# A post-norm decoder layer on one core: scores as 64-row by 32-column tiles of bfloat16 parts, one shared pool of seven PSUM banks

## The chip, the core and the metric

The kernel runs on one NeuronCore of a Trainium2 chip. TensorE multiplies, VectorE (DVE) and ScalarE (ACT) empty PSUM and do the element-wise work, GpSimd (POOL) does masks and small pieces, SyncE (SP) issues DMAs. The metric is device time in microseconds (us) of one execution.

## What is computed

Four sequences of 256 tokens with 128 channels go through self-attention, cross-attention and a small MLP, each followed by a residual add and a layer norm. Both attentions have 16 heads of 8 channels. Cut to what matters:

```python
# 1: latent self-attention, causal over 256 keys
k_eff, v_eff = (W_dq.T @ W_uq.T @ W_uk), (W_uv.T @ W_o.T)      # folded weights
c_kv = x @ W_dkv.T; q = x @ W_dq.T @ W_uq.T
attn = softmax(causal(q_heads @ k_eff @ c_kv.T / sqrt(8)))
x = layernorm(x + heads(attn @ c_kv @ v_eff))
# 2: cross-attention, keys = 512 of memory (ctx) + 256 of x, causal over the 256
q = x @ Wq; k, v = split(concat(mem, x) @ Wkv)
x = layernorm(x + heads(softmax(mask(q @ k.T / sqrt(8))) @ v) @ Wout + bout)
# 3: per-feature MLP: 64 features, 16 inner units each
s = x @ Win + bin_                      # 64 features
h = relu(s[..., None] * W1 + b1)        # 64 x 16
x = layernorm(x + (einsum('btmh,mh->btm', h, W2) + b2) @ Wout + bout)
```

## The kernel before, in words

The work is 8 units: units 0 to 3 are the self-attention of sequences 0 to 3 ("kind 1"), units 4 to 7 their cross-attention ("kind 2"). Each unit has 4 steps, and a step t is one unit and one group of four heads, so there are 32 steps: 16 of kind 1 with 256 keys, 16 of kind 2 with 768 keys.

A step computes its scores twice. First with queries on the partitions ("max", lines 1043 to 1078), so that DVE can take each query's maximum over the keys (lines 866 and 869). The maxima are transposed on TensorE ("shift", line 1084), copied out by ACT (line 744), and sent by two small DMAs (line 600) into two extra rows of the query operand `qm`. Then the scores are computed again with keys on the partitions ("exp", lines 1086 to 1108), where the two extra rows subtract the maximum inside the product, and ACT takes the exponential of each 512-wide bank into `probs` (line 735). Values times weights ("pv", line 1122) are float32 products whose stationary operand is 128 rows by 9 columns (8 channels and a column of ones for the sum); four heads go side by side into the four 32-column strips of the array. ACT copies the result out (`headsT`, line 750, the "drain", one per step), TensorE transposes it by a product ("norm", line 1130), and DVE divides by the sum (lines 888 and 892).

Operand layout of the scores: a head has 8 channels. For accuracy each query and key is split into a high and a low float32r part, and three products of parts are stacked as 3 x 8 rows. Four heads of a group are stacked, which gives 96 rows; `qm` holds for each head a copy with zeros in the rows of the other heads. So a product uses 96 or 98 rows and 128 columns of the array for one head (or, in "exp", streams two heads of queries one after the other). The spreading of the parts over the rows goes through DRAM scratch (`scr_q1`, `scr_k1`, `scr_m`, `scr_q2`, `scr_k2`: written by `put`, lines 530 to 534, read by `take_keys` and `take_queries`, lines 536 to 546).

PSUM has 8 banks: three for "max", two for "exp", one for the heads, two for everything else. The causal masks are bfloat16 products that add a large negative number (lines 1077 and 1108), except in kind 2 of "exp", where GpSimd zeroes the weights (line 669).

The order on all engines comes from a planner, `schedule()` (lines 128 to 354): it simulates the engines with costs per stage and writes one list of stages that every engine walks in order. Ahead of that list stands a prologue written by hand (lines 576 to 595, 715 to 717, 813 to 825, 1015 to 1031): weight folds, the q, k and v products of self-attention, the first memory keys, and memsets of `qm` and `ks` on GpSimd; line 821 prepares an MLP operand on DVE. A step can start once its queries and keys have come back from DRAM. The remaining products of memory are "late" jobs in the list.

The MLP of a sequence: `s` (line 1172) is split into high and low (lines 932 to 936), a selection product copies each feature to its 16 inner units (line 1180), ACT (line 779) or DVE (lines 946 and 951) applies W1, b1 and relu, and lines 1189 and 1197 go back to 128 channels.

## Time and profile before

| | |
|---|---|
| median of 3 runs | 309.77 us (309.51 to 310.59) |
| span of the profiled execution | 309.5 us |
| TensorE (PE) busy | 277.4 us, 90% of the span |
| DVE busy | 234.5 us, 76% |
| ACT busy | 174.3 us, 56% |
| GpSimd busy | 72.6 us, 23% |

In rows of the profile, PE is a matmul and PEld the load of its stationary operand; busy time of a group is the union of its instructions, "mean ns" the length of one including its way through the array, so overlapping instructions make the sum of means larger than the busy time. What stands behind "idle before" is the time the engine waited just before such instructions, and what released it.

### The profile page before, as it was taken

Reading aid. Unit: us, or ns where it says so; the run is one execution under the profiler, and the core shown is the slowest. Engines: PE = TensorE matmul, PEld = TensorE weight load, DVE = VectorE, ACT = ScalarE, POOL = GpSimd, SP = SyncE. Lnnn points to the kernel's source line nnn. Section 1 sums busy time; section 2 is a strip of 40 time slices with the busy share of each in tenths; the row PEclk is TensorE's granted clock in tenths of the full one; section 3 lists DMA queues with packets and bytes.
Section 4 is the critical chain, followed back from the end, with each engine's and each line's share of the span. In section 5 each row is a group of like instructions: output and inputs, shape, how many; then the busy total and the mean of one; then the engine's idle time right before and its main releaser. Section 6 shows DMA issues by size and latency. Waiting matters only on the chain.

```text
span 309.5 us, 6148 instructions
## 1 busy us (share of the span) xinstructions
PE 277.4 (90%) x2240; PEld 181.3 (59%) x2240; DVE 234.5 (76%) x540; ACT 174.3 (56%) x365; POOL 72.6 (23%) x108
## 2 busy tenths in 40 slices
PE   4918678899999999999999999999999999999762
PEld 3706566576776657665656565665665666554431
DVE  2797716587775998888889878799778799777463
ACT  1520235456556567756667566776676658667430
POOL 8996601001202020301111211013101112112211
PEclk9985969999999999999999999999999999999795
DMA  6669999302034512120006200033000000000001
GB/s 188 243 190 303 258 300 229 137 3 55 4 124 85 175 35 102 54 103 3 1 2 162 48 1 2 1 86 71 2 3 2 2 2 1 3 2 17 2 18 34
DMA packets 16109, 23.64 MB, mean 76 GB/s; under 512 B 1648, under 2 KB 11824, under 8 KB 15952
## 3 DMA queue, kind: packets, MB, share of 16 engines
q1 hardware_dynamic: 13632, 14.19, 16.4%
q0 software_dynamic: 2160, 7.47, 8.0%
q10 hardware_dynamic: 288, 1.59, 1.4%
q8 instruction: 18, 0.29, 0.4%
q14 instruction: 11, 0.09, 0.1%
HBM read 13.02 MB, written 9.96 MB: 74 GB/s over the span
## 4 chain that ended last, share of the span: by engine, by line
PE 72%; DVE 17%; DMA 3%; issue 3%; SPq 1%; ACT 1%; POOL 0%; POOLq 0%; ACTq 0%; DVEq 0%
PE psum L1122 15%; PE psum L1104 13%; PE psum L1067 9%; PE psum L1075 7%; DVE pmax L869 5%; PE psum L1077 4%; PE psum L1130 4%; PE psum L1106 4%; DVE w2x L821 3%; DMA qm<-shift_rows 3%; PE psum L1084 3%; PE psum L1108 2%; DVE nmax_s L880 2%; DVE nmax_s L881 2%; PE psum L1159 1%
## 5 line engine op out<-in xcount | busy, mean ns | idle before, releaser
L735 ACT ACTIVATE probs<-psum 128x512 f32<-128x512 f32 x224 | 127.1, 594 | 61.0 <-PE psum L1104 36.1
L869 DVE TENSOR_REDUCE pmax<-psum 128x1 f32<-128x512 f32 (+2 forms) x176 | 111.9, 682 | 19.6 <-PE psum L1067 10.4
L1104 PE MATMUL psum<-qm,ks 98*128 98x512 f32 x176 | 79.9, 463 | 0.0
L1122 PE MATMUL psum<-probs,v 128*9 128x256 f32 (+1 forms) x1024 | 60.6, 354 | 0.0
L1075 PE MATMUL psum<-ks,qm 96*128 96x128 f32 (+1 forms) x256 | 51.0, 309 | 8.2 <-DVE probs L810 8.2
L1067 PE MATMUL psum<-ks,qm 96*128 96x512 f32 x128 | 52.6, 424 | 0.0
L1075 PEld LDWEIGHTS psum<-ks,qm 96*128 96x128 f32 x256 | 43.1, 202 | 13.1 <-issue 9.6
L866 DVE TENSOR_REDUCE nmax<-psum 128x2 f32<-128x512 f32 (+1 forms) x48 | 31.8, 687 | 18.4 <-PE psum L1077 18.3
L1104 PEld LDWEIGHTS psum<-qm,ks 98*128 98x128 f32 x176 | 33.1, 191 | 17.5 <-ACT probs L735 13.3
L669 POOL TENSOR_SCALAR_AFFINE_SELECT probs<-probs 128x512 f32<-128x512 f32 x32 | 19.7, 634 | 96.5 <-ACT probs L735 96.5
L1122 PEld LDWEIGHTS psum<-probs,v 128*9 128x9 f32 x1024 | 21.7, 90 | 31.2 <-issue 9.4
L1077 PE MATMUL psum<-neg,ident_b 128*128 128x256 bf16 (+1 forms) x96 | 31.9, 332 | 0.0
L1106 PE MATMUL psum<-qm,ks 98*128 98x512 f32 x48 | 23.8, 514 | 6.1 <-issue 4.5
L1067 PEld LDWEIGHTS psum<-ks,qm 96*128 96x128 f32 x128 | 24.1, 190 | 4.9 <-DVE pmax L869 1.7
L674 POOL TENSOR_SCALAR vpe<-moments 128x2 f32<-128x2 f32 x12 | 2.6, 218 | 103.5 <-DVE moments L840 103.5
L744 ACT ACTIVATE shift_rows<-psum 8x256 fp32r<-8x256 f32 x32 | 11.8, 368 | 18.2 <-PE psum L1084 14.0
L1130 PEld LDWEIGHTS psum<-wa_sb,headsT 128*128 128x128 f32 x128 | 18.0, 191 | 2.0 <-issue 0.3
L1130 PE MATMUL psum<-wa_sb,headsT 128*128 128x36 f32 x128 | 17.5, 261 | 0.1
L750 ACT ACTIVATE headsT<-psum 128x256 f32<-128x256 f32 x32 | 12.3, 383 | 8.3 <-PE psum L1122 8.1
L1108 PE MATMUL psum<-negT,ident_b 128*128 128x256 bf16 (+1 forms) x48 | 15.9, 332 | 0.0
L1084 PE MATMUL psum<-wa_sb,nmax_s 128*8 128x128 f32 x64 | 12.2, 272 | 2.7 <-DVE nmax_s L881 2.7
L1106 PEld LDWEIGHTS psum<-qm,ks 98*128 98x128 f32 x48 | 9.8, 204 | 8.0 <-issue 5.3
(133 smaller groups left out, 291.4 us busy)
## 6 DMA issues: line engine op xcount, KB each, us to landing
qm<-scr_q SPq DMA_DIRECT2D x28, 96.0 KB
ks<-scr_k SPq DMA_DIRECT2D x6, 384.0 KB, 4.4
ks<-scr_m POOLq DMA_DIRECT2D x2, 768.0 KB, 7.6
ks<-scr_m SPq DMA_DIRECT2D x2, 768.0 KB, 6.4
ctxT_sb<-ctxT ACTq DMA_DIRECT2D x1, 1024.0 KB, 8.2
scr_m<-probs POOLq DMA_DIRECT2D x2, 512.0 KB, 7.1
qm<-shift_rows SPq DMA_DIRECT2D x64, 4.0 KB
scr_k<-split_k SPq DMA_DIRECT2D x4, 256.0 KB, 2.0
```

Of the source, the lines that this page charges most:

```text
L735: nc.scalar.activation(probs[:, ring % PRING, h:h + nh, q0:T], src, ACT.Exp, scale=SCALE).then_inc(exp_done, 1)
L866: nc.vector.tensor_reduce(nmax[:, t % 2, col:col + nh], tile, axis=AX.X, op=ALU.max, negate=True).then_inc(max_done, 1)
L869: nc.vector.tensor_reduce(pmax[:, t % 2, col:col + nh, part], tile, axis=AX.X, op=ALU.max).then_inc(max_done, 1)
L1067: last = nc.tensor.matmul(sk, lhs(j), ks2[0:STACK, b % 2, g, 0:MEM], start=True, stop=True)
L1075: nc.tensor.matmul(o, lhs(j + k), keys, start=(k == 0), stop=False)
L1077: last = nc.tensor.matmul(tile, ident_b[:, :], neg[:, 0:nh, :], start=False, stop=True)
L1084: last = nc.tensor.transpose(m[0:2 * HG, qt * P:(qt + 1) * P], nmax_s[:, t % 2, qt, :], ident)
L1104: nc.tensor.matmul(tbank[n % TBANKS], keys, queries, start=True, stop=True).then_inc(scoresT_ready, 1)
L1106: nc.tensor.matmul(tbank[n % TBANKS], keys, queries, start=True, stop=False)
L1108: nc.tensor.matmul(tile, ident_b[:, :], negT[:, 0:nh, :], start=False, stop=True).then_inc(scoresT_ready, 1)
L1122: last = nc.tensor.matmul(obank[t % OBANKS][32 * j:32 * j + HS + 1, q0:T], v, probs[:, pv_no[s] % PRING, j, q0:T], start=(kt == 0), stop=( ...
L1130: last = nc.tensor.matmul(m[:, qt * HG * (HS + 1):(qt + 1) * HG * (HS + 1)], headsT[:, t % 2, qt * P:(qt + 1) * P], used_rows, start=True, ...
```

## The change

The program is rewritten around the scores:

- Scores. The float32r parts (high, low) become three bfloat16 parts (high, middle, low), and six products of parts are stacked as 6 x 8 = 48 rows, plus three rows for the maximum (in three bfloat16 parts, under ones), so a head takes 51 of 64 rows. Even heads lie on partitions 0 to 63, odd heads on 64 to 127. A score product is issued as four matmuls, each 32 stationary columns wide, into the four column strips of the array (`in_tiles`). No copies padded with zeros are kept.
- "max" becomes "S": a memory unit is one head, 128 queries by 512 keys (4 matmuls); an own unit is one head, both query tiles, 128 + 256 key columns and a 256-column mask (12 matmuls). "exp" becomes "T": one key tile and two heads of the same half, 512 or 256 columns, 8 matmuls, and 4 more for the mask in kind 1.
- "pv" keeps its form: 128 rows, 9 columns, float32.
- PSUM: one bank for the heads, and seven shared by all other stages; the planner assigns the bank and the stage that must be emptied before.
- The splitting of maxima moves from DVE to GpSimd (four small operations a step). "norm" is done once a unit (8 products of 36 columns) instead of once a step. The third part of queries and keys is made on GpSimd. In kind 1 the two row DMAs are issued by ACT, not SP.
- Prologue: most of it is moved into the planned list; only the weight folds stay ahead. The memsets of `qm` and `ks` and the DVE preparation on line 821 are gone. Small filler products ("warm") are added at the start and in planned gaps of TensorE.
- MLP: W1 and b1 become the stationary operand of a float32 product over one 32-row strip (17 rows used), so relu is the only thing left for ACT or DVE, on 512 columns at once.
- A new planner with new costs.

The diff, cut to its core:

```diff
+PARTS = 3
+SLOTS = 6
+STRIP = 32
+HALF = P // 2
+DATA = SLOTS * HS
+ROWS = DATA + PARTS
+FREE_BANKS = 7
+HEADS_BANK = 7
+PRING = 8
+ROWBUFS = 4
...
+LATE = [(("qk", 0), 0), (("qk", 1), 0), (("v1", 0), 0), (("qk", 2), 0), (("v1", 1), 0),
+         (("m", 0), 2), (("vm", 0), 4), (("qk", 3), 6), (("m", 1), 8), (("vm", 1), 10), (("m", 2), 16), (("vm", 2), 17),
+         (("m", 3), 20), (("vm", 3), 21)]
...
+def s_units(t):
+    own = [("own", j, 0) for j in range(HG)]
+    return own if kind(t) == 1 else [("mem", 2 * a + r, qt) for a in range(2) for qt in range(QT) for r in range(2)] + own
...
+                    if what == "qk":
+                        scr = scr_qk[n]
+                        sp.dma_start(scr[:, 0:3, :, :], parts).then_inc(put_done[i], 16)
+                        sp.dma_start(scr[:, 3:5, 0, :], parts[:, 0:4:2, :]).then_inc(put_done[i], 16)
+                        sp.dma_start(scr[:, 3:5, 1, :], parts[:, 3:6:2, :]).then_inc(put_done[i], 16)
+                        sp.dma_start(scr[:, 5, :, :], parts[:, 0::5, :]).then_inc(put_done[i], 16)
...
+                    if i == 0:
+                        sp.dma_start(ctxT_sb[:, :], ctxT).then_inc(ctxT_in, 16)
+                        sp.dma_start(x_sb[:, :, :], x_rows.rearrange("(n p) c -> p n c", p=P)).then_inc(x_in, 16)
...
+                    nc.gpsimd.tensor_copy(high, full).then_inc(max_step, 1)
+                    nc.gpsimd.tensor_sub(rest, full, high).then_inc(max_step, 1)
+                    nc.gpsimd.tensor_copy(mid, rest).then_inc(max_step, 1)
+                    nc.gpsimd.tensor_sub(low, rest, mid).then_inc(max_split, 1)
...
+                    nc.scalar.activation(probs[:, ring % PRING, r, 0:cols], bank_of(s)[:, 0:cols], ACT.Exp,
+                                         scale=SCALE).then_inc(exp_done, 1)
...
+                elif what == "rows" and rows_on_act(s[1]):
+                    send_rows(act, s[1])
...
+                    if src == "mem":
+                        nc.vector.tensor_reduce(pm[:, place, 1 + 4 * qt:2 + 4 * qt], m, axis=AX.X, op=ALU.max).then_inc(reduced, 1)
+                    else:
+                        nc.vector.tensor_reduce(pm[:, place, 2:5], own_blocks(m), axis=AX.X, op=ALU.max).then_inc(reduced, 1)
...
+            def in_tiles(o, lhs, rhs, start, stop):
+                for c in range(HG):
+                    last = nc.tensor.matmul(o[STRIP * c:STRIP * (c + 1)], lhs[:, STRIP * c:STRIP * (c + 1)], rhs, start=start,
+                                            stop=stop, skip_group_check=True)
+                return last
+            def mask(o, r, rows):
+                for c in range(HG):
+                    last = nc.tensor.matmul(o[STRIP * c:STRIP * (c + 1)], half(unit_b, r, HALF), half(rows, r, HALF)[:, c, :, :],
+                                            start=False, stop=True, skip_group_check=True)
+                return last
+            def score(s):
+                queries, keys = (half(qk[:, u % B, p, a, :], r, DATA) for a in range(2))
+                m = bank_of(s)
+                if src == "mem":
+                    return in_tiles(m, queries[:, qt * P:(qt + 1) * P], half(km[:, u % B, p, :], r, DATA), True, True)
+                in_tiles(m[:, 0:P], queries[:, 0:P], keys[:, 0:P], True, False)
+                in_tiles(m[:, P:P + T], queries[:, P:T], keys, False, False)
+                return mask(own_blocks(m)[:, 0:3:2, :], r, neg)
+            def score_pair(s):
+                for a in range(2):
+                    last = in_tiles(m[:, a * (T - q0):(a + 1) * (T - q0)], keys, half(qk[:, u % B, p, 0, q0:], r, ROWS),
+                                    a == 0 or not masked, not masked)
...
+                    elif what == "hid":
+                        for k in range(2):
+                            inner = strip(wb_sb, j, FS + 1)[:, WB["w1"] + k * P:WB["w1"] + (k + 1) * P]
+                            last = nc.tensor.matmul(m[:, k * T:(k + 1) * T], inner, strip(s_sb, j, FS + 1), start=True, stop=True)
-                        last = nc.tensor.matmul(m[:, k * T:(k + 1) * T], sel_r[:, f * P:(f + 1) * P], feat_s[b], start=True, stop=True)
...
-            for s in pro:
-                if s in split_jobs:
-                    low_half(s, bank(pro_bank[s]))
...
-                    for f in range(FG):
-                        last = nc.vector.tensor_scalar(w2x[:, f, :], wb_sb[:, WB["place"] + 32 * f:WB["place"] + 32 * f + 32],
-                                                       wb_sb[:, WB["w2"] + f:WB["w2"] + f + 1], None, ALU.mult)
```

## Rows read from the trace of the kernel before

**Rows 1.** The page: engines over the span, and the chain by engine.

```profile
PE 277.4 (90%) x2240; PEld 181.3 (59%) x2240; DVE 234.5 (76%) x540; ACT 174.3 (56%) x365; POOL 72.6 (23%) x108
PE 72%; DVE 17%; DMA 3%; issue 3%; SPq 1%; ACT 1%; POOL 0%; POOLq 0%; ACTq 0%; DVEq 0%
```

**Rows 2.** Drains (ACT, timeline): start, length; of steps 0, 15 and 31.

```profile
54.79 0.38 ACT L750 ACTIVATE headsT<-psum 128x256 f32<-128x256 f32 x1 [0.20 <-PE psum L1122]
...
121.47 0.38 ACT L750 ACTIVATE headsT<-psum 128x256 f32<-128x256 f32 x1 [0.20 <-PE psum L1122]
...
285.47 0.39 ACT L750 ACTIVATE headsT<-psum 128x256 f32<-128x256 f32 x1
```

**Rows 3.** Windows between those drains: engines busy (instructions), clock, DMA share, GB/s.

```profile
24.00:55.00 31.00, 25.14 (x147) 18.91 (x147) 17.70 (x37) 10.49 (x29) 11.55 (x19) 0.77 0.97 275
55.00:121.50 66.50, 65.31 (x582) 44.95 (x581) 50.84 (x135) 39.27 (x87) 6.41 (x13) 1.00 0.26 79
121.50:285.50 164.00, 161.46 (x1378) 100.61 (x1378) 138.93 (x307) 110.34 (x217) 27.62 (x50) 1.00 0.10 27
285.50:309.50 24.00, 13.30 (x88) 7.93 (x88) 11.42 (x40) 7.24 (x16) 4.57 (x10) 0.75 0.06 17
```

**Rows 4.** TensorE timeline within a kind 2 step: start, length, instructions merged.

```profile
203.47 0.40 PE L1104 MATMUL psum<-qm,ks 98*128 98x512 f32 x1
203.71 0.40 PE L1067 MATMUL psum<-ks,qm 96*128 96x512 f32 x1
204.04 0.84 PE L1122 MATMUL psum<-probs,v 128*9 128x256 f32 x16
204.81 0.50 PE L1104 MATMUL psum<-qm,ks 98*128 98x512 f32 x1
205.14 0.40 PE L1067 MATMUL psum<-ks,qm 96*128 96x512 f32 x1
```

**Rows 5.** Those pv instructions (line 1122), window 203 to 205: min/median/max ns.

```profile
L1122 PE MATMUL psum<-probs,v x16: 272/326/385, 204.0 to 204.6; 128*9 128x256 f32 x8, 128*9 128x128 f32 x8
```

**Rows 6.** Groups by shape: busy us, mean ns of one, idle before.

```profile
L735 ACT ACTIVATE probs<-psum 128x512 f32<-128x512 f32 x224 | 127.1, 594 | 61.0 <-PE psum L1104 36.1 <-PE psum L1108 23.1
L869 DVE TENSOR_REDUCE pmax<-psum 128x1 f32<-128x512 f32 x128 | 81.8, 682 | 10.8 <-PE psum L1067 10.4
L1077 PE MATMUL psum<-neg,ident_b 128*128 128x256 bf16 x64 | 18.8, 294 | 0.0
L1130 PE MATMUL psum<-wa_sb,headsT 128*128 128x36 f32 x128 | 17.5, 261 | 0.1
L1077 PE MATMUL psum<-neg,ident_b 128*128 128x512 bf16 x32 | 13.1, 408 | 0.0
L880 DVE CAST nmax_s<-nmax 128x8 fp32r<-128x8 f32 x32 | 9.5, 297 | 1.1
```

**Rows 7.** The two waits of TensorE's sequencer ahead of that pv pair (line 1116), window 203.2 to 203.5.

```profile
L1116 PEldq EVENT_SEMAPHORE  x2: 51/51/51, 203.3 to 203.4; - x2
```

**Rows 8.** A 256-column float32 product in the chain: start, share of the chain in us.

```profile
83.45 0.43 PE psum L1159 x2
```

**Rows 9.** The prologue and the first exponential (timeline): start, length.

```profile
4.08 0.38 ACTq L699 DMA_DIRECT2D wb_sb<-wb  x1
8.81 0.38 ACT L713 ACTIVATE probs<-psum 128x256 fp32r<-128x256 f32 x1 [2.56 <-PE psum L1004]
12.01 11.51 DVE L821 TENSOR_SCALAR w2x<-wb_sb 128x32 f32<-128x32 f32 x8
26.16 0.69 DVE L866 TENSOR_REDUCE nmax<-psum 128x4 f32<-128x512 f32 x1 [0.59 <-PE psum L1077]
41.57 1.26 ACT L735 ACTIVATE probs<-psum 128x512 f32<-128x512 f32 x2 [5.84 <-PE psum L1108]
```

**Rows 10.** DMA issues on the page: count, KB each, us from issue to landing.

```profile
ks<-scr_k SPq DMA_DIRECT2D x6, 384.0 KB, 4.4
ctxT_sb<-ctxT ACTq DMA_DIRECT2D x1, 1024.0 KB, 8.2
```

1766 lines of the change are left out of this document (844 added, 922 removed).

## Prediction, written before the changed kernel was run

> **What bounds the kernel now.** I read the page first. TensorE is busy 90% of the span and carries 72% of the chain that ended last, DVE 17% [rows 1]. That busy time includes the way through the array, so it must be checked stage by stage. The drains mark the stages: the first ends a start-up of 54.8 us, the sixteenth comes at 121.5, the thirty-second at 285.5, and 24.0 us follow [rows 2]. Between them the windows show the load [rows 3]:
>
> - start-up, up to 54.8 us: nobody is full but the DMA engines, 0.97 of their time at 275 GB/s from 24 to 55 us, at a TensorE clock of 0.77 granted;
> - kind 1, 15 steps in 66.7 us, 4.45 us each: TensorE 65.3 of 66.5 us, DVE 50.8, ACT 39.3;
> - kind 2, 16 steps in 164.0 us, 10.25 us each: TensorE 161.5, DVE 138.9, ACT 110.3;
> - tail, 24.0 us, a chain of small stages.
>
> So per step of kind 2 TensorE needs 10.1 us, DVE 8.7, ACT 6.9 (the row divided by 16). TensorE is the bound, but DVE stands only 15% below: removing TensorE work can bring a step down to DVE's 8.7 and no further. The sum is made against the profiled span of 309.5 us; the median of the runs is 309.8, so I add 0.3.
>
> **What a score costs on TensorE.** 512 columns of float32r follow each other at 0.24 us (203.47 to 203.71) [rows 4]. The bfloat16 masks cost 294 ns for 256 columns and 408 for 512 [rows 6]; the difference, 0.114 us per 256 columns, is the same rate. So going to bfloat16 gains nothing per column: all gain must come from two heads at once, one in each half of the rows. Columns in a kind 2 step: before, 8 x 512 (memory), 2560 (own, with masks) and 11 x 512 (exp) = 12288. After: S 8 x 512 + 4 x 640, T 10 x 512 + 2 x 256 = 12288 again. At 0.114 us per 256 that is 5.5 us if the halves take turns, 2.75 us if they always overlap.
>
> Do they overlap? For column strips rows show it: the 16 pv instructions take 272 to 385 ns each, 326 in the median [rows 5], 5.2 us one after another, and all lie within 0.84 us [rows 4]. Row halves are not used before, so their overlap is bounded from both sides, 0 and 100%. I take 85%: it is the same kind of tile as the strips, S and T units alternate between halves in the planned order and each has a bank of its own; and the overlap regulates itself, because when TensorE is late more banks are empty and more pairs can go together. The other 15% is for units that wait for a bank or have a stage of another form between them. Score time after: 5.5 x (1 - 0.85/2) = 3.2 us. Before: 19 x 0.24 + 2560 columns (1.1) = 5.7 us. Saved: 2.5 us a step.
>
 Taking 0.2 us for each (they share the way with pv when adjacent), +0.5 us; bounds 0 and 0.75 for as many, 2.5 us for eight more.
>
> **pv** is unchanged. **norm**: the same 128 instructions, 17.5 us [rows 6], in eight lumps instead of 32; nothing. **Shift**: at most as long as before; nothing.
>
> **MLP on TensorE.** 16 selections of 2 x 256 columns in float32r (0.23 us) become float32 products; one of 256 columns takes 0.43 us [rows 8], so a pair 0.86, or 0.43 if K of 17 rows makes it cheaper; +0.2 to +0.63 us for each of four a unit. Taken +0.4 us a step.
>
> Kind 2 on TensorE: 10.1 - 2.5 + 0.5 + 0.4 = 8.5 us, bounds 8.0 (full overlap, no more switches) and 11.5 (no overlap, 2.3 us: 10.8; and the larger switch and MLP values).
>
> **DVE.** Reduced columns are the same: 128 memory units as before, 81.8 us for 128 [rows 6], 0.64 each; own units are 128 x 384 instead of 96 x 512, equal columns, 32 instructions more, each of which adds the fixed part of one (0.64 minus 512 columns; taking a quarter, 0.11 us), 3.5 us in all. The split of the maxima leaves DVE: 9.5 us on line 880 [rows 6] and as many instructions on line 881; each norm saves little. Relu is one instruction of 512 columns (before, four of 256 on DVE) and can go to ACT. Net -1 us a step in kind 2 before balancing, but DVE also waits less in start-up and can run ahead of T in kind 1. Per step: 7.7 to 8.7 us. The split on GpSimd lengthens the way from the last maximum to the rows by about 1 us; GpSimd is busy 27.6 of 164 us [rows 3], and T lags S by several steps' worth of banks, so it is hidden; if that cover is gone it costs 1 us a step in kind 1 only.
>
> **ACT.** Exponentials: 224 of 512, 127.1 us [rows 6], 0.567 each; after, 192 of 512 (108.9) and 64 of 256. The latter cost 0.567 minus half its columns, 0.30: 19.2. Sum 128.1, +1.0 us. Kind 1 adds two DMA issues a step at 0.38 [rows 9], 0.8 us, to ACT's 39.3/15 = 2.6: 3.4, still below 4.2. In kind 2 ACT takes most copies of the MLP: 6.9 + 1 = 7.9 us.
>
> So in kind 2 all three stand between 7.7 and 8.7 us. Three engines that near to each other do not reach 100% of the largest; before, with one clear bound, the step was 10.25 against 10.1. I take **9.1 us a step**, 16 x 9.1 = 146 us (bounds 8.5 and 9.9).
>
> **Kind 1.** Before, the scores of a step are 2560 + 2048 columns (with masks), 2.05 us, and some 0.3 us of loads; after the same columns at 85%: 1.2 us; -1.2. Switches +0.4. Work that stood ahead of step 0 and now lies in the list (three qk, two v1, one m, one vm: 14 products of 256 columns at 0.43 [rows 8], 6 us): +0.4. GpSimd makes third parts there, off the path. 4.45 - 1.2 + 0.8 = 4.05; taken **4.2** for the row traffic through DRAM; 15 x 4.2 = 63 us (bounds 3.9 and 4.6).
>
> **Start-up.** Before: first split copy 8.8 us, then DVE is held 11.5 us by line 821 while GpSimd clears memory; first maximum 26.2; first exponential 41.6, behind a saturated DMA; first drain 54.8 [rows 9, 2, 3]. After: ACT copy at 8.8, high, left and low parts 2.5 us, four puts of 0.4 to 0.6 us on SP: 13.5. Landing 4.4 [rows 10]: 18. The take is queued behind ctxT and x on SP's queue; ctxT alone took 8.2 us to land [rows 10], so 4.4 to 8.2 us: 23. Four S units 2.6, split on GpSimd 1, shift and copy 0.6, two issues 0.8, landing 2 to 4.4, T of step 0 1.8, pv 0.7: **33 us** (bounds 30 and 39). The saturated stretch thins out, because 3 of the 4 units' operands are no longer sent before step 0.
>
> **Tail.** Before 24.0 us. norm is 12 products longer (+1.3 us at 17.5/128 each), the MLP's split and second relu pass go (-2 to -4 us): **22 us** (20 to 24).
>
> **Sum.** 33 + 63 + 146 + 22 = 264 us. Own range of this case: 30 + 58.5 + 136 + 20 = 245 to 39 + 69 + 158 + 24 = 290.
>
> **Rivals.**
>
> *The halves take turns* (slower). If a product in one half of the rows waits for the one in the other, kind 2 needs 5.5 instead of 3.2 us for scores, 8.5 + 2.3 = 10.8 and with the same loss on top 11.4 us; kind 1 4.2 + 0.9 = 5.1. 33 + 15 x 5.1 + 16 x 11.4 + 22 = 314 us. Every 10 points of overlap are worth 0.275 x 16 + 0.1 x 15 = 6 us, so the kernel turns slower only when overlap is under about 10%. Against it: strips do overlap [rows 4, 5]. For it: no row has two row halves. Chance 0.12. The Trainium skill (TensorEngine Tiling (Array Packing), Key Properties) says that tiles run independently and that a change of tiling mode drains the array; the second agrees with the gaps around pv, the first no row here shows for row halves.
>
> *TensorE's instructions cannot be supplied.* A kind 2 step grows to about 225 products of scores and pv, with as many loads, some 470 instructions (before 1378 x 2 / 16 = 172 [rows 3]). The densest stretch, pv, runs 32 instructions from 204.04 to 204.81, 24 ns each [rows 4]; were that the supply and not the columns, 470 x 0.024 = 11.3 us a step, kind 1 6.2: 33 + 93 + 181 + 22 = 329 us. Against it: the two waits ahead of the two halves of a pv pair, between which 16 instructions are handed on, start at 203.3 and 203.4 [rows 7], under 0.2 us for 16, below 13 ns each; 470 of them are 6 us. Chance 0.05. The Trainium skill (TensorE: Matmul & The Clock Gate, "Wait — 56ns, not 53.3ns?") says that without hardware decode the sequencer spends about 62 ns per matmul; by that figure 225 products would be 14 us a step, an estimate from the page that these waits speak against.
>
> *Switches and order.* The scores gain as forecast, but the list changes form so often (some eight more visits a step at 0.3 us) that TensorE stays the bound at 10.3 us in kind 2 and 4.9 in kind 1: 33 + 73.5 + 165 + 24 = 295 us. Chance 0.11.
>
> *Better balance.* Full overlap, engines at 98% of DVE: 8.5 and 3.9 us a step: 31 + 58.5 + 136 + 20 = 245 us, down to 238 with a quicker start. Chance 0.12.
>
> **How the numbers follow.** Forecast 0.58 (264, 245 to 290), better balance 0.12 (238 to 250), switches 0.11 (288 to 308), halves in turns 0.12, supply 0.05, all gains cancelling to within 0.3% 0.02. The range 244 to 300 holds the forecast's case and most of the two beside it. 0.3% (0.9 us) is about what a measurement of this kernel tells from no change. Faster: 0.58 + 0.12 + 0.11 = 0.81, less 0.01: 0.80; same 0.02; slower 0.18.
>
> **What would show it.** Right: the first drain near 33 us; S units of even and odd heads starting within some 30 ns of each other and their columns lying over each other; DVE near 90% busy in kind 2; a step of 9.1 us. Wrong on overlap: the second of two neighbouring S units starts 0.2 us after the first. Wrong on supply: matmuls of one unit spaced over 20 ns with nothing waited for. Wrong on start-up: rows or takes landing after 30 us with DMA full. Wrong on the clock: less than 1.00 granted inside the steps, which would double every TensorE term there; before it was 1.00 from 55 to 285 us, 0.77 ahead and 0.75 in the tail [rows 3].

## The result and the profile after

| | before | after |
|---|---|---|
| median | 310.18 us | 295.48 us (293.45 to 299.06) |
| ratio, 95% interval | | 0.9481 [0.9413, 0.9549] |
| span of the profiled execution | 309.5 us | 291.7 us |
| start-up (to the first drain) | 54.8 us | 51.7 us, forecast 33 |
| kind 1 (to the sixteenth) | 66.7 us | 76.5 us, forecast 63 |
| kind 2 (to the thirty-second) | 164.0 us | 141.3 us, forecast 146 |
| tail | 24.0 us | 22.2 us, forecast 22 |

The kernel is 5.2% faster, by 14.7 us, where 46 were forecast. It lies inside the range, 31 us above the forecast; the profiled execution, on which the stages below are read, is 27.7 us above it (291.7 against 264). Executions of one program differ by 3.5 to 12 us, the longer ones at a lower mean clock (280.5 us at 0.93 and 287.7 at 0.90 for the fastest version), so medians are over all executions and the intervals over the fast ones.

Names used from here on: a product of the list is called by its operand and sequence, `qk` n for queries and keys (0 to 3 self-attention, 4 to 7 cross-attention), `m` n and `vm` n for keys and values of memory; a "put" writes its parts to DRAM scratch, a "take" reads them back spread over the rows, "the rows" are the two small DMAs with the maxima of a step. Page, chain, drains and windows of after, which answer [rows 1], [rows 2] and [rows 3]:

```profile
PE 241.0 (83%) x5973; PEld 144.2 (49%) x5973; DVE 194.3 (67%) x429; ACT 159.8 (55%) x367; POOL 99.8 (34%) x250
PE 42%; DVE 19%; DMA 14%; SPq 9%; issue 7%; ACT 3%; POOL 3%; ACTq 2%; POOLq 0%; DVEq 0%
51.66 0.36 ACT L782 ACTIVATE headsT<-psum 128x256 f32<-128x256 f32 x1
128.21 0.38 ACT L782 ACTIVATE headsT<-psum 128x256 f32<-128x256 f32 x1
269.48 0.38 ACT L782 ACTIVATE headsT<-psum 128x256 f32<-128x256 f32 x1
24.00:51.70 27.70, 15.60 (x474) 10.21 (x474) 14.03 (x33) 6.09 (x15) 9.17 (x26) 0.65 0.94 215
51.70:128.20 76.50, 60.87 (x1710) 39.18 (x1693) 46.16 (x109) 38.45 (x99) 26.41 (x77) 0.93 0.43 103
128.20:269.50 141.30, 134.95 (x3605) 73.11 (x3586) 114.64 (x237) 104.72 (x236) 44.86 (x115) 0.96 0.18 41
269.50:291.70 22.20, 14.71 (x135) 10.33 (x134) 10.23 (x34) 5.53 (x13) 4.56 (x10) 0.94 0.06 19
```

TensorE has 36 us less work, but its share of the chain fell from 72 to 42%: DMA, SP's queue and "issue" (time for which the profile shows no wait) now hold 30%. The granted clock, 1.00 through both attentions before [rows 3], is 0.93 and 0.96. The loss is in the first two stages, and there in what is not arithmetic.

Where TensorE is supplied, the change does what the forecast says. Its timeline in kind 2, answering [rows 4]:

```profile
225.40 0.29 PE L1011 MATMUL psum<-qk,km 51*32 51x256 bf16 x4
225.42 0.28 PE L1011 MATMUL psum<-qk 48*32 48x256 bf16 x4
225.51 0.28 PE L1011 MATMUL psum<-qk,km 51*32 51x256 bf16 x4
225.53 0.28 PE L1018 MATMUL psum<-neg,unit_b 64*32 64x256 bf16 x4
```

A T unit and an S unit of the other row half start 0.02 us apart, and their next products, 0.11 us later, 0.02 us apart again: each half takes its 256 columns in 0.11 us, both at once. The Trainium skill (TensorEngine Tiling (Array Packing), Key Properties) says that different tiles load and multiply in parallel; these rows agree.

The chain of the start-up (start, length, what), where the forecast had the last put issued at 13.5 us, the puts landed at 18, the take at 23 and the rows at 30:

```profile
9.69 2.75 DVE ident_b L836
12.94 0.91 DVE qk L591
15.86 0.33 SPq L633
18.21 0.49 SPq L643
21.99 1.16 SPq L636
24.19 9.03 DMA qk<-scr_qk
35.70 1.55 PE psum L1135 x2
38.56 1.36 ACTq L599
39.95 4.56 DMA qk<-shift_rows
```

DVE casts constants and clears a tile first, so the first put leaves at 15.9. It has landed at 19.6, but SP issues ctxT (L643), x, the biases and the second put before the first take, which leaves at 23.3. That take needs 9.0 us to land, at 33.2, with the DMA engines 0.94 busy. A memory product (L1135) stands ahead of the shift, and the rows land at 44.5, after 4.6 us.

Every wait of 1.5 us or more that TensorE has between 60 and 200 us (start and length of what runs after it, and in brackets the wait):

```profile
83.87 0.39 PE L1011 MATMUL psum<-qk 48*32 48x128 bf16 x16 [4.10 <-DMA qk<-scr_qk]
91.24 0.54 PE L1011 MATMUL psum<-qk 48*32 48x256 bf16 x12 [3.16 <-issue]
97.96 0.30 PE L1011 MATMUL psum<-qk 48*32 48x256 bf16 x3 [2.60 <-issue]
163.37 1.23 PE L1086 MATMUL psum<-probs,v 128*9 128x128 f32 x9 [2.11 <-issue]
166.99 0.40 PE L1011 MATMUL psum<-qk,km 51*32 51x256 bf16 x4 [1.85 <-DMA qk<-shift_rows]
```

The granted clock is at half (1.2 of 2.4 GHz) from 19.6 to 36.7 us, 43.5 to 50.3, 84.5 to 87.9, 91.3 to 94.7, 98.1 to 101.5, 163.0 to 173.2, and again from 289.3 in the tail: up to 173.2 each time within or right behind one of these pauses or of those of the start-up. Windows around the second (columns as in [rows 3]):

```profile
84.00:88.00 4.00, 4.00 (x140) 2.37 (x133) 2.93 (x7) 1.20 (x4) 0.78 (x4) 0.57 1.10 222
88.00:91.30 3.30, 0.14 (x12) 0.06 (x15) 0.23 (x1) 0.93 (x2) 0.00 (x0) 1.00 0.42 122
91.30:95.00 3.70, 3.70 (x121) 2.33 (x124) 1.48 (x4) 1.41 (x4) 0.78 (x4) 0.54 1.04 192
```

So three questions: do the halves carry what they seem to; what holds start-up and kind 1; what are the pauses marked "issue".

### The profile page after: what moved, and what is told of

Same layout as the page of the kernel before. It is cut to its first block, busy times and chain, and to the rows that moved or that the text cites. A ratio compares the mean times of both kernels' runs of the same rounds, so it can differ in the third digit from the quotient of the medians.

```text
span 291.7 us, 13772 instructions
## 1 busy us (share of the span) xinstructions
PE 241.0 (83%) x5973; PEld 144.2 (49%) x5973; DVE 194.3 (67%) x429; ACT 159.8 (55%) x367; POOL 99.8 (34%) x250
## 4 chain that ended last, share of the span: by engine, by line
PE 42%; DVE 19%; DMA 14%; SPq 9%; issue 7%; ACT 3%; POOL 3%; ACTq 2%; POOLq 0%; DVEq 0%
PE psum L1011 13%; PE psum L1086 10%; DVE pm L869 9%; DMA qk<-shift_rows 6%; DMA qk<-scr_qk 5%; DVE pm L871 4%; PE psum L1106 4%; PE psum L1018 3%; PE psum L958 3%; ACTq L599 2%; ACT probs L774 2%; DMA scr_m<-spl 2%; SPq L635 1%; PE psum L1173 1%; SPq L634 1%
## 5 line engine op out<-in xcount | busy, mean ns | idle before, releaser
L774 ACT ACTIVATE probs<-psum 128x512 f32<-128x512 f32 (+1 forms) x256 | 120.6, 554 | 41.6 <-PE psum L1011 20.9
L1011 PE MATMUL psum<-qk 51*32 51x128 bf16 (+3 forms) x2048 | 63.2, 266 | 31.7 <-DMA qk<-scr_qk 20.9
L871 DVE TENSOR_REDUCE pm<-psum 128x3 f32<-128x384 f32 x128 | 63.5, 550 | 36.6 <-PE psum L1018 36.5
L869 DVE TENSOR_REDUCE pm<-psum 128x1 f32<-128x512 f32 x128 | 79.1, 681 | 7.0 <-PE psum L1011 7.0
L1011 PEld LDWEIGHTS psum<-qk 48*32 48x32 bf16 (+1 forms) x2048 | 35.2, 96 | 56.1 <-DMA qk<-scr_qk 21.5
L1011 PE MATMUL psum<-qk,km 51*32 51x256 bf16 x1024 | 37.9, 278 | 2.8 <-DMA qk<-shift_rows 2.5
L1086 PEld LDWEIGHTS psum<-probs,v 128*9 128x9 f32 x1024 | 23.2, 91 | 26.0 <-issue 13.8
L1011 PE MATMUL psum<-km,qk 48*32 48x512 bf16 x512 | 35.6, 394 | 0.2
L1018 PE MATMUL psum<-neg,unit_b 64*32 64x256 bf16 x512 | 31.5, 305 | 0.0
L1011 PEld LDWEIGHTS psum<-qk,km 51*32 51x32 bf16 x1024 | 15.3, 92 | 18.9 <-issue 5.5
L1018 PE MATMUL psum<-negT,unit_b 64*32 64x256 bf16 x256 | 16.5, 299 | 0.0
```

What stands on the lines that cost most here:

```text
L774: nc.scalar.activation(probs[:, ring % PRING, r, 0:cols], bank_of(s)[:, 0:cols], ACT.Exp, scale=SCALE).then_inc(exp_done, 1)
L869: nc.vector.tensor_reduce(pm[:, place, 1 + 4 * qt:2 + 4 * qt], m, axis=AX.X, op=ALU.max).then_inc(reduced, 1)
L871: nc.vector.tensor_reduce(pm[:, place, 2:5], own_blocks(m), axis=AX.X, op=ALU.max).then_inc(reduced, 1)
L1011: last = nc.tensor.matmul(o[STRIP * c:STRIP * (c + 1)], lhs[:, STRIP * c:STRIP * (c + 1)], rhs, start=start, stop=stop, skip_group_check=True)
L1018: last = nc.tensor.matmul(o[STRIP * c:STRIP * (c + 1)], half(unit_b, r, HALF), half(rows, r, HALF)[:, c, :, :], start=False, stop=True, sk ...
L1086: last = nc.tensor.matmul(heads[STRIP * j:STRIP * j + HS + 1, q0:T], v, weights, start=(k == 0), stop=(k == len(key_tiles(t)) - 1))
```

## Experiments

Spans and stages are those of the profiled execution. Differences of 2 us between single profiles prove nothing; the place and the releaser of a single wait can be compared. Versions stand against the kernel before on the same chip, 310.1 to 310.7 us.

### The row halves

**one_half**: every score, and every mask, reads rows 0 to 63 (the diff shows the queries; keys and masks change likewise). It leaves out the scores of the odd heads.

```diff
-                queries, keys = (half(qk[:, u % B, p, a, :], r, DATA) for a in range(2))
+                queries, keys = (half(qk[:, u % B, p, a, :], 0, DATA) for a in range(2))
```

> All score products (S and T) read rows 0 to 63, so neighbouring units can no longer lie side by side in the two halves of the rows; the scores of odd heads are those of the even heads, everything else is as in the changed kernel. If the halves do overlap as the prediction took it, score time per kind 2 step rises from about 3.2 us to 5.5 and TensorE becomes the bound: from step 19 to 31 (8.2 us a step in the changed kernel) I expect 10 to 11 us a step and 25 to 45 us more in all. If the halves already took turns, nothing changes: 8.2 us a step and the same total within 1%.

Measured: 345.98 us, span 344.2, clock 0.799; kind 1 94.2 us, kind 2 169.8.

```profile
180.00:220.00 40.00, 38.69 (x664) 23.57 (x658) 23.18 (x47) 19.10 (x42) 6.53 (x19) 0.70 0.26 52
40.00:80.00 40.00, 40.00 (x744) 25.59 (x736) 21.20 (x48) 13.65 (x32) 14.04 (x41) 0.50 0.17 45
```

Reading one half alone costs 50 us (345.98 - 295.48, one execution), more than the whole gain: without the second half the kernel is slower than before. Only part of that is turns. Steps at full clock are about 1 us longer (steps 22, 23 and 27: 8.8 against 7.7, 8.7 against 7.4, 8.6 against 7.8), half of the 2.3 us that the forecast gave to turns. The other part is the clock, at half for 138 us of the span against 47 us in after, although the records show TensorE busy all through stretches such as the second above; that alone can be up to 46 us. The price of "halves take turns" in the forecast, 314, was too low because it counted no clock.

### The start-up

**ctx_late**: the reads of ctxT, x and the biases behind the first take instead of ahead of it.

```diff
-                    if i == 0:
-                        sp.dma_start(ctxT_sb[:, :], ctxT).then_inc(ctxT_in, 16)
...
+                    if i == 0:
+                        sp.dma_start(ctxT_sb[:, :], ctxT).then_inc(ctxT_in, 16)
```

> The loads of ctxT, x and the biases are issued after the first take instead of before it. If the first score waits (34.0 us) because its take is queued behind 1.5 MB of other loads, the first S comes 4 to 7 us earlier and the whole is 3 to 6 us shorter (some is given back at the later DMA wait of unit 3). If the wait is only for the puts and for SP's issues, less than 2 us change.

Measured: 293.07 us, ratio 0.9507 [0.9393, 0.9621]. The take leaves at 20.6 us instead of 23.3 and lands in 7.0 us instead of 9.0. First maximum at 28.9 us instead of 34.1, first exponential at 44.0 instead of 45.4, first drain at 49.7 instead of 51.7.

**start2**: ctx_late, and the casts of constants and the second memset on DVE behind the low parts of the first product.

> As ctx_late, and the casts of the identity and the second memset of DVE come behind the first low parts instead of ahead of them. If DVE's constants (9.7 to 13.9 us, slowed by GpSimd's memsets) hold the first put, it leaves some 3 to 4 us earlier (12 instead of 15.9 us) and the first S starts near 25 us (34.0 in the changed kernel, 28.9 with ctxT late). If the puts then only wait for the weights and x, nothing moves against ctx_late. In the total, 2 to 6 us below the changed kernel, because the rows of the first step still land behind the traffic of units 1 and 2.

Measured: 292.63 us, 0.9354 [0.9302, 0.9406]. The put leaves at 13.8 us instead of 15.9, the first maximum is at 28.4; first exponential 44.6, first drain 49.9. TensorE waits 3.5 us (35.2 to 38.6) for the take of the next unit, behind the second shift; for ctxT, ahead of m0, it waits 0.4 us only. The cast that stood first is short here, where GpSimd is no longer clearing memory (the line of after, then of start2):

```profile
9.61 2.82 DVE L836 CAST ident_b<-wa_sb 128x128 bf16<-128x128 f32 x1
13.65 0.22 DVE L837 CAST ident_b<-wa_sb 128x128 bf16<-128x128 f32 x1
```

**qk4_ctx**: ctx_late on qk4_early (below), with m0 at step 4 instead of 2.

> qk4_early with ctxT, x and the biases read behind the first take instead of ahead of it, and the first product of memory (m0) moved from score step 2 to step 4, so that it does not stand ahead of the first shift. With ctxT late alone the first S unit ran at 28.9 us instead of 34.1, but the first T only at 44.0 instead of 45.4 and the first drain at 49.7 instead of 51.7; in the combination with late constants m0 made TensorE wait 3.5 us for ctxT ahead of the shift. Theory (the rest of the gain was lost to m0 waiting for ctxT in the list): first T at 38 to 41 us, first drain at 44 to 47, span 3 to 5 us under that of qk4_early. Rival (the rows of the maximum land late because 3 MB of takes and ctxT are in the DMA engines then, whatever the order): rows land 7 us or more after their issue, first T at 42 us or later, first drain 48 to 50, span 0 to 2 us under qk4_early.

Measured: 301.98 us, 0.9618 [0.9569, 0.9668]; first maximum 28.4, first exponential 43.4, first drain 51.7; kind 1 66.3 and kind 2 155.0, against 61.4 and 150.4 without it. With m0 out of the way TensorE still waits 3.0 us for the next take.

Four orders (combo below is the fourth) bring the first maximum to 28.0 to 28.9 us and none brings the first exponential below 43.2. What is put off falls on the next take or on the rows: these orders only choose who waits. What remains is the volume (0.94 of the DMA engines for 28 us); no run cut it, so that is argued and not shown.

### Kind 1

The planner counts 2.3 us for a put or a take to land; on the page of after they take 5.1 and 6.4. It puts the product of the fourth operand (qk3) at score step 11, though it may come from step 6. SP's queue shows the rest: put at 71.4, take at 76.4, landed at 83.8, while DVE has no maximum to take from 66.6 to 84.4 us, and all exp units of steps 8 to 11 (and of step 7 all but the first) stand behind the first S unit of step 12 in TensorE's list.

**lands**: landing times of the planner's costs set to measured ones.

```diff
-           ... "put_lands": 2300, "take_lands": 2300, "rows": 900, "rows_land": 2200
+           ... "put_lands": 5100, "take_lands": 6500, "rows": 900, "rows_land": 3500
```

> The planner is told what the trace shows for landings: 5.1 us for a put and 6.5 us for a take (2.3 each before), 3.5 us for the rows (2.2 before). It then puts the T units of steps 6 to 9 ahead of the first S unit of unit 3 in TensorE's order. If the loss of kind 1 is TensorE waiting at the head of its order for a take while work behind it is ready, kind 1 gets 5 to 12 us shorter and the total 4 to 12. If DMA volume is the bound of kind 1, the same wait turns up elsewhere and the total changes by less than 1%.

Measured: 294.88 us, 0.9454 [0.9293, 0.9614]; kind 1 72.7, kind 2 144.4, tail 24.2. True costs alone gave 4 us in kind 1 and took 7.5 elsewhere (start-up 2.4, kind 2 3.1, tail 2.0).

**qk3_early**: qk3's product is taken first once step 6 is reached, costs as they were.

```diff
+PRESSED = (("qk", 3),)
...
+                if s in PRESSED:
+                    best.append((min(start_of(s), now) if start_of(s) < NEVER and ready(s) <= now else start_of(s), -1, n, s))
```

> The planner is made to place the q and k product of unit 3 as soon as its step gate (6) opens, instead of in the gap that it finds at step 11. If the 17 us in which DVE has no S unit (67 to 84 us) and the three pauses of TensorE at 80, 88 and 95 us come from that late product and its 7 us take, they disappear: no idle stretch of DVE over 5 us between 60 and 100 us, and kind 1 takes 66 to 70 us instead of 76.5. The total falls by 4 to 9 us. If the rows or ACT bound kind 1, only the idle time moves and the total stays within 1%.

Measured: 287.19 us, 0.9257 [0.9214, 0.9299]; kind 1 72.6, kind 2 138.8, span 285.2. All three pauses of 80 to 98 us are gone; one of 2.8 us, for a take, came at 62.7, and this one:

```profile
104.36 1.04 PE L1015 MATMUL psum<-km,qk 48*32 48x512 bf16 x12 [6.48 <-DMA qk<-scr_qk]
```

S of step 16 waits for qk4, whose take stands in SP's queue behind a take of memory; the clock is at half from 100.0 to 110.2 us.

**combo** (start2 with qk3_early) and **combo_lands** (that with lands):

> start2 and qk3_early together, planner costs as they were. If start-up and kind 1 are separate losses, their gains add: 6 to 14 us below the changed kernel, 281 to 289 us. If the second only gives back what the first gained (both limited by the same DMA volume), the total is that of the better one.

Measured: 287.93 us, 0.9291 [0.9236, 0.9345], first maximum 28.0, first drain 52.1; with the landing times as well 294.7, 0.948 [0.9404, 0.9556]. Gains in the start-up and in kind 1 do not add: against qk3_early the first drain is even 0.6 us later.

**qk4_early**: qk3_early, with qk4 pressed as well and the memory products m1 and m2 not before steps 17 and 19.

> On top of the version that plans the fourth query-and-key product of self-attention early (285.2 us profiled, 287.2 median): the first cross-attention product (qk4) gets the same preference, and the memory products m1, vm1, m2, vm2 may come only from score steps 17 and 19 on, so that their puts and takes (1.5 MB a take) do not stand ahead of qk4's take in the queue of SP. In the version without this, TensorE stood from 97.9 to 104.4 us for that take, which landed 9.2 us after it was issued, right behind another take. Theory (the queue ahead of the take is what makes it late): qk4's take lands in 6 to 7 us, the pause falls from 6.5 us to 3 or 4 and with it part of the half-clock stretch of 10 us after it; span 281 to 283 us. Rival (the take is late because x1T of unit 0 comes late, since TensorE's list puts all scores of kind 1 ahead of it; the transfers do not matter): the pause stays at 5 us or more, span 285 to 287. A third way: the later memory products delay step 20, shown by a new pause of more than 1.5 us between 145 and 175 us; then 286 to 290.

Measured: 287.7 us, 0.9256 [0.9213, 0.93]. **Kind 1 61.4 us**, below the forecast's 63, with no pause over 1.7 us. Some of that is work moved to kind 2: m2 and vm2 (2.1 us of TensorE, at 103.1 and 116.6 in after) and the puts and takes of m1 and m2, which come from 114.0 us on. The rest of the 15.1 us is the place of products and transfers in the two lists. But kind 2 took 150.4. Besides the moved work and 13.7 us at half clock (145.3 to 159.0) there are two pauses:

```profile
145.60 0.61 PE L1015 MATMUL psum<-qk,km 51*32 51x256 bf16 x7 [3.36 <-issue]
152.84 1.04 PE L1015 MATMUL psum<-qk,km 51*32 51x256 bf16 x24 [3.24 <-DMA qk<-shift_rows]
```

### Kind 2

**rows_act**: in kind 2, too, ACT and not SP issues the rows (`rows_on_act` returns True).

> The two row DMAs of every step, kind 2 too, are issued by ACT. If the stall of TensorE at 159 to 167 us comes from SP, which waits for the landing of a put before it can issue the rows queued behind, the stall goes and the whole is 5 to 8 us shorter. If it comes from full DMA engines, the rows land as late from ACT's queue and the total stays within 1%. ACT itself gets 0.8 us a step more, below its bound.

Measured: 303.88 us (294.83 to 305.53). The wait for the rows at 167 us is gone, but in the profile (305.24 us) kind 2 took 150.2 us, with the clock at half at 178, 188 and from 246.6 to 256.8 us, the last with no pause of 1 us near it. Whether the DMA issues on ACT brought this about is not shown: of four executions one took 294.83, as long as after.

**m1_early**: qk4_early, with m1 pressed from step 10, m2 from 20, m3 from 23.

> As qk4_early, but the memory products are spread over the queue of SP: m1 with preference from score step 10 (put and take then lie in kind 1, well ahead of qk4's), m2 from step 20 and m3 from step 23. In qk4_early kind 1 took 61.4 us and kind 2 150.4, with two pauses of TensorE at 142 and 150 us (6.6 us) and 13.7 us at half clock: put and take of m1 and the put of a query-and-key job stood in SP's queue (130 to 140 us) ahead of the rows of the next step. In the version where they were not there, kind 2 took 138.8. Theory (both halves are free of each other, the loss is the place in the queue alone): kind 1 61 to 64 us, kind 2 137 to 141, span 273 to 278. Rival (m1's transfers in kind 1 delay the rows or qk3 there as they did in kind 2): kind 1 66 to 70 us, span 279 to 284.

Measured: 293.63 us, 0.9426 [0.9291, 0.9562]; kind 1 70.8, kind 2 151.3, with this in it:

```profile
153.09 1.07 PE L1015 MATMUL psum<-qk,km 51*32 51x256 bf16 x32 [6.33 <-DMA qk<-shift_rows]
```

My theory fell on both counts. No take of memory was near; the rows of step 19 stood behind a take of qk7 that waited for its own put (last part issued at 140.6, take at 146.1, rows at 147.0), and then landed behind it. That also explains the rows in qk4_early, in SP's queue:

```profile
139.24 1.01 SPq L640 DMA_DIRECT2D scr_qk<-spl  x1
145.60 0.84 SPq L659 DMA_DIRECT2D qk<-scr_qk  x2
146.48 1.49 SPq L603 DMA_DIRECT2D qk<-shift_rows  x2
```

**takes_behind**: qk4_early with three takes moved in the list behind rows.

```diff
+    for late, mark in ((("take", "m", 2), ("rows", 19)), (("take", "qk", 7), ("rows", 20)), (("take", "m", 3), ("rows", 21))):
+        plan.remove(late)
+        plan.insert(plan.index(mark) + 1, late)
```

> qk4_early with three entries of the list moved and nothing else: the takes of m2, qk7 and m3 (needed only at steps 24, 28 and 28) stand behind the rows of steps 19, 20 and 21 in SP's queue instead of ahead of them. In qk4_early the take of qk7 waited for its put to land (put at 137.7 us, take at 145.6) and the rows of step 19 behind it were issued at 146.5; TensorE paused 3.4 and 3.2 us at 142 and 150 and ran 13.7 us at half clock. The m1_early run kept these rows behind a take although no transfer of memory was near, and had the same pause (6.3 us at 147). Theory (what costs kind 2 is a take that waits for its put and holds the rows behind it; neither the volume nor the product): no pause over 1.5 us between 140 and 156, kind 1 61 to 63 us as before, kind 2 138 to 142, span 274 to 278. Rival (kind 2 is longer because kind 1 left it more work: memory products and later queries): the pauses go or move, kind 2 stays at 146 or more, span 282 to 286.

Measured: **282.26 us** (280.47 to 287.7), 0.9147 [0.8981, 0.9314], the fastest version; its median is 5.4 us below that of qk4_early, though the intervals of the ratios overlap and the two profiles differ by 1.2 us only. The wait for rows is gone. Kind 1 60.5 us, kind 2 148.3: together 208.8, the forecast's 209, with one term under and the other over (217.8 in after, 211.4 in qk3_early, 211.8 in qk4_early). Kind 2 is not the 138 to 142 that I expected: three pauses marked "issue" remain there (134.3, 150.3 and 157.1 us; 1.8, 2.0 and 2.6 us).

### The pauses marked "issue"

TensorE's instructions themselves come by DMA. The page, queue of instructions, of the kernel before and then of after:

```profile
q8 instruction: 18, 0.29, 0.4%
```

```profile
q8 instruction: 47, 0.77, 1.2%
```

They are packets of 16 KB that take 1.1 us in the median. I set each pause of TensorE of 1 us or more whose releaser is "issue", in all 18 profiles of this study, beside the last packet that came in before its end, from the trace's DMA records:

```
                 pause (us)        last packet in at   resumed after
before           36.05 to 40.52    38.66               1.87
after            88.08 to 91.24    89.81               1.43
after            95.36 to 97.96    96.63               1.33
after           161.26 to 163.37  161.73               1.64
takes_behind    150.25 to 152.25  150.71               1.54
takes_behind    157.10 to 159.73  158.42               1.31
all 39 pauses                                          1.19 to 1.90
```

In the changed kernels one packet comes in every 4.6 to 5.6 us in the median (14.5 before); by chance the last column would spread over all of that. All 39 end 1.2 to 1.9 us after one. Of the 58 pauses of 1 us or more after 20 us that have another releaser only 12 do.

The same records show what makes a packet late. In 34 of the 39 cases the DMA engines were at least 0.75 busy with other transfers in the 2 us before the packet began; of all 800 packets after 30 us this holds for 199. A packet itself is hardly longer with data in flight (1.4 us in the median against 1.0), and many of these packets begin just as a full stretch ends: in after the takes fill the engines until 88.9 us, and the packet of the second pause begins at 88.89. So what comes late seems to be the start of the fetch; this rests on these counts and on the one pause that the next experiment made.

**extra_dma**: takes_behind, with 7 reads of 1 MB into an unused tile, after the drains of steps 22 to 28, where there are no transfers.

```diff
+                    if 22 <= t < 29:
+                        if t > 22:
+                            act.wait_ge(extra_in, 16 * (t - 22))
+                        act.dma_start(extra[:, :, 0:256], ctxT[:, 0:2048].rearrange("p (n c) -> p n c", c=256)).then_inc(extra_in, 16)
```

> takes_behind with one addition: after each of the drains of steps 22 to 28 ACT issues a read of 1 MB of ctxT into a tile nobody uses, in rows of 1 KB like the takes. In takes_behind this stretch (175 to 262 us) has a DMA share of 0.02, no pause of TensorE over 0.6 us and steps of 6.7 to 9.4 us. Every longer pause of TensorE with no releaser seen so far (3.2, 2.6 and 2.1 us in the changed kernel; 3.4, 3.6, 2.3 in its variants; 4.5 us in the kernel before) lay over the fetch of a packet of 16 KB in the queue of instructions, which moves through the same 16 DMA engines, and nearly all lay where these were busy with takes. Theory (TensorE's instructions come late when data transfers fill the DMA engines, and the changed kernel fetches 47 such packets where the kernel before fetched 18): pauses of 1 to 3.5 us marked as issue appear between 180 and 250 us, each over an instruction packet, with stretches at half clock behind them; kind 2 longer than 148.3 us by 4 to 15 us, span 289 to 300. Rival (the packets are where the pauses are by chance, one comes every 4.5 us; the pauses come from waits that the profile does not show): no pause of over 1 us there, except a wait for rows that land late, kind 2 within 2 us, apart from 7 issues of 0.4 us on ACT; span 284 to 288.

Measured: 294.55 us (286.42 to 296.7), span 293.6, kind 2 158.4 (expected: 4 to 15 us more than 148.3). Up to the drain of step 21 the two profiles differ by 1 us in kind 2; from there, where the reads are, extra_dma takes 11 us more. Its shortest execution, at a mean clock of 0.94, is 6 us above the shortest of takes_behind. Two stretches of takes_behind, then the same of extra_dma, and the pause that is new:

```profile
190.00:205.00 15.00, 14.93 (x428) 8.32 (x414) 13.60 (x27) 11.06 (x27) 4.10 (x12) 1.00 0.02 5
220.00:235.00 15.00, 14.65 (x410) 8.09 (x407) 14.03 (x28) 9.82 (x23) 2.81 (x10) 1.00 0.02 6
```

```profile
190.00:205.00 15.00, 13.44 (x268) 8.06 (x252) 8.70 (x18) 6.56 (x15) 2.08 (x7) 0.69 0.40 131
220.00:235.00 15.00, 12.09 (x344) 5.85 (x336) 10.00 (x19) 8.73 (x21) 3.04 (x8) 0.89 0.43 137
226.91 1.58 PE L1101 MATMUL psum<-probs,v 128*9 128x256 f32 x16 [2.69 <-issue]
```

One pause marked "issue", of 2.7 us, ending 1.47 us after a packet, and one wait of 1.35 us for rows (194.1 us), followed by 13.7 us at half clock from 195.6: 17 us of half clock in a stretch that had none. Background transfers lengthened steps 23, 24 and 26 by 2.3, 4.3 and 4.1 us. Only one of seven reads delayed a packet so that TensorE ran dry; that packet began at 224.5, as the read's full stretch (221 to 224) ended. That pauses would appear at each read, as expected, was too much.

### The half clock

**fill_rows**: qk4_early with 18 filler products directly ahead of the first exp unit, where TensorE pauses for the rows.

```diff
+        if s == ("T", 0, 0, 0):
+            k = min(range(FREE_BANKS), key=lambda k: (free_at[k], -k))
+            plan.append(("warm", 18, k, holder[k]))
```

> The run before with one addition: 18 filler products of 256 bfloat16 columns (about 2 us at full clock) directly ahead of the first exp unit (T of step 0), where TensorE otherwise pauses for the rows of the maximum from about 42.8 to 44.5 us and then runs at half clock from 43.5 to 50.3. Nothing else in the list changes. Theory (a pause of TensorE is what the half clock follows, and it costs the columns of 7 us twice): the stretch after 43 us is gone or under 2 us long, first drain 2 to 3 us earlier than without the fillers although these cost up to 1 us, span about 2 us shorter. Rival (the half clock there has another cause, or what bounds the stretch is ACT's exponentials): the stretch stays or goes with no effect, first drain the same or up to 1 us later.

Measured: 287.15 us, 0.924 [0.9198, 0.9282], span 283.8. The half clock at 43 us is gone and the first drain is at 50.8 us instead of 52.3; another stretch of the same length came at 53.3 us, behind a pause marked "issue".

**behind_fill** (takes_behind with the fillers), and **best** (m1_early with them, 290.96 us, 0.9378 [0.9272, 0.9483], first drain 57.1):

> takes_behind with the 18 filler products ahead of the first exp unit. On qk4_early they took away the half-clock stretch at 43 us and gave 2.4 us of span; on m1_early the first drain came 5 us later with them (57.1 against 51.8) and kind 1 was 10 us shorter, so their effect is not settled. Theory (a pause filled saves half of the slow stretch that follows it): first drain 50 to 51.5 us, span 1 to 3 us under that of takes_behind. Rival (spread of the start-up from execution to execution is as large as the effect): first drain anywhere from 50 to 57, medians of the two within 1.5 us.

Measured: 291.09 us, 0.937 [0.9156, 0.9584], first drain 57.2; against 282.26 without. With the fillers the first drain came once 1.5 us earlier and twice 3 to 5 us later. What the half clock costs by itself is not settled by fillers: their effect is inside the spread of the start-up (first drain 52.3 in qk4_early and 54.0 in takes_behind, whose lists are the same there).

## Why the forecast was wrong, point by point

- **What bounds the kernel; columns.** Right. The masks and scores go at 0.11 us per 256 columns, both halves at once. TensorE's busy time per step of kind 2 is 8.4 us (134.95 / 16), forecast 8.5.
- **DVE, ACT, norm.** Right in sign, both too dear:

```profile
L774 ACT ACTIVATE probs<-psum 128x512 f32<-128x512 f32 x192 | 102.2, 609 | 24.4 <-PE psum L1011 16.9 <-PE psum L1018 5.9 <-PE psum L1086 1.1
L774 ACT ACTIVATE probs<-psum 128x256 f32<-128x256 f32 x64 | 22.7, 389 | 17.2 <-PE psum L1018 12.9 <-PE psum L1011 4.0
L869 DVE TENSOR_REDUCE pm<-psum 128x1 f32<-128x512 f32 x128 | 79.1, 681 | 7.0 <-PE psum L1011 7.0
L871 DVE TENSOR_REDUCE pm<-psum 128x3 f32<-128x384 f32 x128 | 63.5, 550 | 36.6 <-PE psum L1018 36.5
```

  Exponentials sum to 124.9 us (forecast 128.1), and ACT needs 6.5 us a step of kind 2 (forecast 7.9). The maxima cost what was forecast: 79.1 us for 512 columns (81.8) and 63.5 for 384 (three quarters of 81.8 and 3.5, 64.9). DVE still needs only 7.2 us a step of kind 2 and is 81% busy there, not near 90%: under my 7.7 to 8.7, the difference lies in its other work.
- **Kind 2, 16 x 9.1 = 146.** The term held, 8.83 a step, but partly by luck: a loss that I had taken did not come, and one that I had not seen did (two pauses, 4.0 us, and 10.2 us at half clock in steps 19 and 20). Steps 20 to 31, nearly undisturbed, take 8.2 us, below my lower bound of 8.5: TensorE needs less, and in the last nine of them it alone is near its limit:

```profile
197.00:269.50 72.50, 71.06 (x1943) 38.17 (x1936) 58.39 (x122) 57.41 (x131) 21.28 (x56) 1.00 0.02 6
```

  TensorE is 98% busy there, DVE and ACT 81 and 79%, so three engines near each other was not the case.
- **Kind 1, 15 x 4.2 = 63.** The smaller of the two failed steps is "taken **4.2** for the row traffic through DRAM". The products of the stage fit the sum (60.5 and 61.4 us were reached, with 2.1 us of work moved out), but I costed the prologue's products, now in the list, only by their 6 us of TensorE. Moved into an in-order list, each also issues a put and a take, and whoever stands behind it waits, on SP as on TensorE. Price: 13.5 us, of which the pauses are 9.9 (4.10 + 3.16 + 2.60) and the half clock behind them up to half of 10.2 us. Two of the three pauses are late instruction packets; that these, too, went when qk3 was placed earlier is measured, why is not.
- **Start-up, 33 us.** The larger failed step is the chain "13.5 ... Landing 4.4 ... 18 ... 23" and what follows it, mis-sized by 18.7 us. The last put was issued by 18.2 instead of 13.5: 4.7. Of this, 2.5 us came back in start2, where the casts and the second memset of DVE stand behind the low parts; 2.0 of the rest is ACT's first split copy, at 10.8 instead of the 8.8 taken from the kernel before. The puts landed at 19.6, in 1.4 us instead of 4.5: -3.1. Then SP held the take until 23.3, since it issues three reads and four writes first: 3.7, in no term. The take needed 9.9 us from there instead of 5: 4.9. Maxima, shift and rows 11.3 instead of 7 (half clock, m0 in front, rows 4.6): 4.3. T and pv of step 0, 7.2 instead of 3, nearly all at half clock: 4.2. "The saturated stretch thins out" was the wrong sentence: the share went from 0.97 to 0.94, and none of the four orders tried frees it.
- **Tail, 22 us.** 22.2. (12 products at 17.5/128 each are 1.6 us and not the 1.3 of the sum; it changes nothing.)
- **Rivals.** Halves in turns: did not happen; would have been 346, not 314. Supply: wrong as posed, matmuls of one unit start 3 to 4 ns apart (225.40 us); right in another form, since they must be fetched and the fetch comes late behind data, 7.9 us of pauses in after (3.16 + 2.60 + 2.11). "Switches and order" at 295 named nearly the measured time, by a mechanism that is not there: it wanted TensorE full at 10.3 us a step of kind 2, and it is busy 8.4 of 8.8.
- **Clock.** It stood under what would make the forecast wrong, with no price. That was the missing rival: 27 us of half clock between 43 and 174 us. The Trainium skill (TensorE: Matmul & The Clock Gate, HAM oscillation — how this bites in real kernels) describes kernels whose waits for DMA drop the clock again and again. The rows agree for most pauses; a pause of 2.0 us in after (up to 55.0 us) and one of 1.8 in takes_behind (up to 136.1) were followed by none. In one_half the clock was at half with TensorE busy 40.00 of 40 us, and from 281.0 to 298.1 with no wait of 0.3 us in the 20 us before, which no pause explains. What decides there stays open.

In short: the gain came from the place where it was forecast, two row halves at once, and 32 us of start-up and kind 1 that the sum did not hold took most of it back (18.7 and 13.5, less 4.7 in kind 2).

What is still open: the profile of takes_behind is 21 us above the forecast (285.0 against 264), all of it in the start-up (54.0 against 33); and what half a clock costs in a stretch where TensorE is not alone on the path.

## What to carry to other kernels

When a prologue becomes part of an in-order list, cost each moved step by all that it puts on every queue, and by who stands behind it there; a take that waits for its put must not stand ahead of a transfer that is due sooner, which here was worth 5 us by the medians; the place of one product in the list was worth 7 to 8. When the work of the bounding engine shrinks and its instructions multiply, count the instruction fetches and look at what else the DMA engines carry. Give a falling clock a price of its own in the sum wherever an engine that was full before will wait.

## What the runs showed of the hardware that I had not expected

- TensorE's instructions arrive in packets of 16 KB through the same DMA engines as data, 47 in this kernel and 18 before. A late packet stopped TensorE for 1.0 to 4.5 us, and it resumed 1.2 to 1.9 us after the packet was in; 34 of 39 such packets began behind 2 us in which the DMA engines were 0.75 busy or more. The profile calls it "issue".
- After pauses of TensorE of 1.35 us (extra_dma, 194.1) and 2.0 us (takes_behind, 152.3) the granted clock was at half for 13.7 and 3.4 us, and after one of 1.8 us (takes_behind, 136.1) not at all. In one_half, with tiled products in one half of the rows, it was at half from 18.2 to 89.9 us, 57.5 of the last 57.9 of them with TensorE recorded busy.
- Two small DMAs of 3 KB, issued by 159.3 us between takes of 1.5 MB in one queue, released TensorE only at 167.0, 7.7 us later; in the start-up they took 4.6 us.
- A DVE cast of 128 columns took 2.82 us while GpSimd cleared memory (after, 9.61 us; its two memsets end at 12.35), and 0.22 us in start2 without.
